# Spectral image tower with a token part: attention on all partitions, column-grouped gate logits, and GpSimd adding up the experts

## The reference

```python
h = ln(h + softmax(q @ k.T / 8) @ v)                   # attention inside one image of 64 tokens
h = ln(h + y1)   # 8 experts of 64-256-64, the best one a token, gate = softmax, capacity 1.25
h = ln(h + mingru(mingru(h)))                           # gated linear recurrence along the 64 rows
h = ln(h + ln(h + y2) * gamma + beta)                   # 16 experts of 64-128-64, the best two a token
```

## Time and profile before

| | us |
|---|---|
| median of three runs | 3008.84 |
| the profiled execution | 3009.09 |
| its span in the profile | 3007.3 |
| token part in the span (2557.6 to 3007.3) | 449.7 |
| TensorE busy in the span | 2714.3 |
| VectorE busy | 2113.5 |
| ScalarE busy | 1992.8 |
| GpSimd busy | 69.6 |

### The profile page before, as it was taken

One profiled execution on the slowest core, in us unless ns is written; L12 is line 12 of the kernel. 1 busy time (PEld: TensorE's weight loads), 2 busy tenths in 40 slices (PEclk: granted clock), 3 DMA queues, 4 the chain that ended last, 5 costly groups with the idle time before them and its releaser, 6 DMA issues.

```text
span 3007.3 us, 75958 instructions
## 1 busy us (share of the span) xinstructions
PE 2714.3 (90%) x28706; PEld 1588.6 (53%) x28706; DVE 2113.5 (70%) x4206; ACT 1992.8 (66%) x2415; POOL 69.6 (2%) x93
## 2 busy tenths in 40 slices
PE   5777789999898999898999879999999999999994
PEld 3444456666666666565666653444444443664441
DVE  5999777888676888676888755445454443677877
ACT  5888666677565777565677546777777777455551
POOL 0000000000000000000000002000000000100000
PEclk9999999999999999999999999999999999989996
DMA  3422255744454744364744344311111110114243
GB/s 93 135 108 106 82 192 171 239 175 174 147 181 153 242 177 174 128 209 156 233 177 177 134 153 90 86 36 60 50 49 58 38 60 0 30 30 102 54 85 64
DMA packets 160241, 361.59 MB, mean 120 GB/s; under 512 B 45878, under 2 KB 123734, under 8 KB 124246
## 3 DMA queue, kind: packets, MB, share of 16 engines
q1 hardware_dynamic: 136982, 185.95, 21.0%
q10 hardware_dynamic: 18432, 134.23, 11.0%
q0 software_dynamic: 4672, 39.20, 6.0%
HBM read 204.77 MB, written 154.53 MB: 119 GB/s over the span
## 4 chain that ended last, share of the span: by engine, by line
PE 74%; DVE 9%; issue 6%; ACT 6%; DMA 4%; SPq 1%; ACTq 0%; DVEq 0%; POOL 0%; POOLq 0%
PE pA L1514 16%; PE pT L1609 8%; PE pA L1522 8%; PE pS L1551 7%; PE pD L1598 5%; PE pD L1565 4%; PE pT L1540 3%; PE pD L1485 3%; PE pD L1580 3%; PE pA L1540 2%; DVE arena L1881 2%; PE pT L1619 2%; ACT h_rows L1698 2%; PE pA L600 2%; DMA h_scratch<-h_new 1%
## 5 line engine op out<-in xcount | busy, mean ns | idle before, releaser
L1848 DVE TENSOR_REDUCE small<-arena 128x32 f32<-128x1056 f32 x320 | 396.7, 1241 | 321.2 <-ACT arena L1683 317.7
L1514 PEld LDWEIGHTS pA<-conv_bd,h_in 128*128 128x128 f32 x4096 | 482.1, 193 | 108.8 <-issue 108.8
L1514 PE MATMUL pA<-conv_bd,h_in 128*128 128x128 f32 x4096 | 520.5, 281 | 3.0 <-DVE arena L1841 1.7
L1673 ACT COPY w_sb<-pA 128x1024 f32<-128x1024 f32 x256 | 259.5, 1014 | 252.7 <-PE pA L1522 235.3
L1694 ACT ACTIVATE h_new<-pT,bet,gam 128x1024 f32<-128x1024 f32 x256 | 307.3, 1200 | 152.7 <-PE pT L1540 135.3
L1862 DVE SCALAR_TENSOR_TENSOR w_sb<-w_sb,small 128x1024 f32<-128x1024 f32 x320 | 385.7, 1209 | 2.1
L1683 ACT ACTIVATE arena<-w_sb 128x1024 f32<-128x1024 f32 x320 | 338.5, 1058 | 10.2
L1551 PEld LDWEIGHTS pS<-cst,h_new 128*128 128x128 f32 x2048 | 220.6, 141 | 203.7 <-issue 133.4
L1540 PE MATMUL pT<-cst,w_sb 128*128 128x128 f32 x2048 | 278.7, 280 | 39.6 <-DVE w_sb L1862 20.0
L1551 PE MATMUL pS<-cst,h_new 128*128 128x128 f32 x2048 | 280.6, 280 | 24.2 <-ACT h_new L1694 21.7
L1540 PEld LDWEIGHTS pT<-cst,w_sb 128*128 128x128 f32 x2048 | 233.5, 144 | 104.4 <-DVE w_sb L1862 48.9
(11 more groups left out here) (316 smaller groups left out, 3421.3 us busy)
## 6 DMA issues: line engine op xcount, KB each, us to landing
h_scratch<-h_new ACTq DMA_DIRECT2D x128, 1024.0 KB, 4.4
h_in<-h_scratch SPq DMA_DIRECT2D x128, 1024.0 KB, 5.0
w_sb<-gates_scratch SPq DMA_DIRECT2D x168, 128.0 KB, 6.9
y_scratch<-w_sb POOLq DMA_DIRECT2D x32, 576.0 KB, 8.5
y_in<-y_scratch SPq DMA_DIRECT2D x512, 36.0 KB
w_sb<-in_L_tok_w1r_dram POOLq DMA_DIRECT2D x8, 576.0 KB, 6.9
w_sb<-in_L_tok_w1i_dram POOLq DMA_DIRECT2D x8, 576.0 KB, 6.7
w_sb<-in_L_tok_w2r_dram POOLq DMA_DIRECT2D x8, 576.0 KB, 7.2
```

Source lines behind the costliest of these rows:

```text
L1514: pe.matmul(pA[:, c:c + 128], h_in[:, 1024 * n + c:1024 * n + c + 128], conv_bd[:], start=(j == 0), stop=False, skip_group_check=True)
L1848: dve.reduce_sum(var[n], sq[n % 2], axis=AX).then_inc(s["summed"], 1)
```

## The change

It does four things. Queries, keys, values and transposed weights are laid on 128 partitions: the two halves of each 128-token tile for queries and keys, even and odd tiles for values and weights, so that each needs 512 columns. Gate logits are computed in a new step `gq` with the gate weights, padded to 32 columns, as the stationary side, in four column groups of 256 columns; ScalarE copies them, and `gl` turns them with two transposes. GpSimd makes the additions of the sum over experts; there are four buffers `Z3`, VectorE waits for a buffer and, ahead of the bias, for the last addition, by a new semaphore `added`; the clear at L891 goes. The list of steps is another one. In `ADDS` the n-th expert in the list has the number of its addition.

```diff
@@ -177,18 +177,18 @@
 TOKEN_ORDER = """
-    xt1.0 qkv.0 xt1.1 sc.0 ex.0 qkv.1 pt.0 xt1.2 pv.0 qkv.2 xt1.3 xt2.0 sc.1 ex.1 sc.2 ex.2 gl1.0 pt.1 gx1.0 pt.2 cum.0 pv.1 qkv.3
-    gt1.0 e1.0 pv.2 e1.0 e1.0 xt2.1 e1.0 xt2.2 e1.0 e1.0 sc.3 gl1.1 e1.0 ex.3 gx1.1 e1.0 eb1.0 pt.3 wg.0 cum.1 gl1.2 yb1.0 pv.3
-    gt1.1 e1.1 e1.1 xt3.0 e1.1 gx1.2 gru0.0 xt2.3 e1.1 gru1.0 e1.1 gback.0 cum.2 e1.1 e1.1 xt4.0 gl1.3 gl2.0 gx2.0 gm2.0 e1.1
-    eb1.1 gt2.0 e2.0 e2.0 e2.0 e2.0 e2.0 e2.0 e2.0 yb1.1 e2.0 e2.0 gx1.3 e2.0 e2.0 xt3.1 e2.0 gru0.1 e2.0 cum.3 gru1.1 gt1.2 e2.0
-    e2.0 e2.0 gt1.3 e1.2 gback.1 e1.2 eb2.0 e1.2 e1.2 yb2.0 e1.2 e1.2 e1.2 e1.2 eb1.2 xt4.1 e1.3 e1.3 yb1.2 e1.3 e1.3 xt3.2 e1.3
-    gru0.2 gl2.1 e1.3 gru1.2 gx2.1 gm2.1 e1.3 gback.2 gt2.1 e1.3 e2.1 eb1.3 xt4.2 e2.1 e2.1 e2.1 yb1.3 e2.1 gl2.2 e2.1 e2.1 xt3.3
-    e2.1 gx2.2 gm2.2 e2.1 e2.1 gru0.3 e2.1 e2.1 e2.1 e2.1 gru1.3 gt2.2 e2.1 e2.1 gback.3 e2.2 e2.2 e2.2 e2.2 e2.2 eb2.1 xt4.3 e2.2
-    e2.2 gl2.3 e2.2 e2.2 e2.2 gx2.3 gm2.3 e2.2 e2.2 e2.2 e2.2 gt2.3 e2.2 e2.2 eb2.2 e2.3 yb2.1 e2.3 e2.3 e2.3 e2.3 e2.3 e2.3 yb2.2
-    e2.3 e2.3 e2.3 e2.3 e2.3 e2.3 e2.3 e2.3 e2.3 eb2.3 yb2.3
+    xt1.0 xt1.1 qkv.0 sc.0 ex.0 qkv.1 pt.0 wg.0 pv.0 sc.1 xt1.2 xt1.3 qkv.2 xt2.0 sc.2 gq1.0 gl1.0 ex.1 pt.1 gx1.0 cum.0 pv.1
+    qkv.3 gt1.0 e1.0 xt2.1 e1.0 gq1.1 e1.0 gl1.1 gx1.1 e1.0 ex.2 e1.0 pt.2 sc.3 e1.0 pv.2 e1.0 e1.0 cum.1 eb1.0 ex.3 xt2.2 pt.3
+    gt1.1 e1.1 yb1.0 e1.1 e1.1 pv.3 gq1.2 xt3.0 e1.1 gru0.0 gl1.2 e1.1 gru1.0 e1.1 gback.0 e1.1 xt2.3 gx1.2 xt4.0 cum.2 gq2.0
+    gq1.3 gl2.0 gx2.0 gm2.0 e1.1 eb1.1 gt2.0 e2.0 e2.0 e2.0 e2.0 e2.0 gl1.3 e2.0 yb1.1 gx1.3 cum.3 gt1.2 e2.0 e2.0 e2.0 e2.0 xt3.1
+    e2.0 e2.0 gru0.1 e2.0 e2.0 e2.0 gru1.1 e2.0 eb2.0 e1.2 e1.2 yb2.0 e1.2 e1.2 e1.2 gback.1 gt1.3 e1.2 e1.2 e1.2 eb1.2 xt4.1 e1.3
+    e1.3 yb1.2 e1.3 e1.3 xt3.2 e1.3 gru0.2 gq2.1 e1.3 gru1.2 gl2.1 e1.3 gx2.1 gm2.1 e1.3 gback.2 gt2.1 e2.1 e2.1 e2.1 eb1.3 xt4.2
+    e2.1 e2.1 e2.1 gq2.2 e2.1 e2.1 e2.1 gl2.2 e2.1 gx2.2 yb1.3 e2.1 e2.1 e2.1 gm2.2 e2.1 xt3.3 e2.1 e2.1 gt2.2 gru0.3 e2.2 e2.2
+    e2.2 gru1.3 e2.2 e2.2 e2.2 gback.3 e2.2 e2.2 e2.2 e2.2 xt4.3 e2.2 e2.2 gq2.3 e2.2 gl2.3 eb2.1 gx2.3 gm2.3 e2.2 e2.2 e2.2 gt2.3
+    eb2.2 e2.3 e2.3 e2.3 yb2.1 e2.3 e2.3 e2.3 e2.3 yb2.2 e2.3 e2.3 e2.3 e2.3 e2.3 e2.3 e2.3 e2.3 e2.3 eb2.3 yb2.3
 """
-TOKEN_SENDS = dict(xt1=(0, 2), qkv=(4, 2), sc=(1, 0), pt=(0, 2), pv=(1, 0), xt2=(2, 0), xt4=(2, 0), gl1=(1, 0), gl2=(1, 0), cum=(1, 0),
+TOKEN_SENDS = dict(xt1=(0, 2), qkv=(2, 1), sc=(1, 0), pt=(0, 1), pv=(2, 0), xt2=(2, 0), xt4=(2, 0), gq1=(0, 1), gq2=(0, 1), gl1=(1, 0), gl2=(1, 0), cum=(1, 0),
                    wg=(0, 1), gt1=(0, 1), gt2=(0, 1), eb1=(1, 0), eb2=(1, 0), xt3=(0, 2), gru0=(1, 1), gru1=(1, 1), gback=(1, 0),
                    yb1=(1, 0), yb2=(1, 0),
...
-        b2a, b2b, ge2 = param(P, S), param(P, S), param(P, 512)
+        b2a, b2b, ge2, z3c, z3d = param(P, S), param(P, S), param(P, 512), param(P, 512), param(P, 512)
-        gwa, gwb = param(P, E1), param(P, E2)
+        gwa, gwb = param(P, 32), param(P, 32)
...
-        QT, KT, VB, PT = ([arena[0:64, 2048 * i + 1024 * j:2048 * i + 1024 * j + 1024] for j in range(2)] for i in range(4))
+        QT, KT, VB, PT = ([arena[:, 1024 * i + 512 * j:1024 * i + 512 * j + 512] for j in range(2)] for i in range(4))
-        Z3 = [w_sb[:, 2 * CW + CW * i:3 * CW + CW * i] for i in range(2)]
+        Z3 = [w_sb[:, 2 * CW + CW * i:3 * CW + CW * i] for i in range(2)] + [z3c, z3d]
...
+        LG = [y_in[:, 512:768], cst[:, 128:384]]
-        GT_PLACE, EB_FREED, sends_d = {}, {}, 0
+        GT_PLACE, EB_FREED, ADDS, sends_d = {}, {}, [], 0
+            if key[0] in ("out1", "out2"):
+                ADDS.append(ADDS[-1] + (key[2] > 0) if ADDS else -1)
...
             def qkv(c):
                 pe.wait_ge(s["ones_set"], 2)
                 taken("s", "xt1", c)
-                for j in range(2):
-                    for which, w in (("d", wq), ("s", wk)):
-                        b = bank(which)
-                        sent(which, pe.matmul(b[0:64, :], w, XT[:, 1024 * c + 512 * j:1024 * c + 512 * j + 512], start=True, stop=True))
-                for j in range(2):
-                    b = bank("d")
-                    for i in range(8):
-                        a = 1024 * c + 512 * j + S * i
-                        mm = pe.matmul(b[0:64, S * i:S * i + S], XT[:, a:a + S], wv, start=True, stop=True)
-                    sent("d", mm)
+                for which, w in (("d", wq), ("s", wk)):
+                    b = bank(which)
+                    x = XT[:, 1024 * c:1024 * c + 1024].rearrange("p (t h q) -> p h t q", h=2, q=S)
+                    for h in range(2):
+                        mm = pe.matmul(b[64 * h:64 * h + 64, :].rearrange("p (t q) -> p t q", q=S), w, x[:, h], start=True, stop=True)
+                    sent(which, mm)
+                b = bank("d")
+                for m in range(4):
+                    for h in range(2):
+                        for u in range(2):
+                            a = 1024 * c + 256 * m + 128 * u + 64 * h
+                            q = 128 * m + 64 * h
+                            mm = pe.matmul(b[64 * u:64 * u + 64, q:q + 64], XT[:, a:a + S], wv, start=True, stop=True)
+                sent("d", mm)
             def sc(c):
                 taken("d", "qkv", c)
...
-                        a = 128 * i + 64 * h
-                        mm = pe.matmul(b[64 * h:64 * h + 64, S * i:S * i + S], QT[c % 2][:, a:a + 64], KT[c % 2][:, a:a + 64], start=True, stop=True)
+                        q, a = slice(64 * h, 64 * h + 64), slice(S * i, S * i + S)
+                        mm = pe.matmul(b[q, a], QT[c % 2][q, a], KT[c % 2][q, a], start=True, stop=True)
             def pt(c):
-                for j in range(2):
-                    b = bank("s")
-                    for i in range(4):
-                        t = CT * c + 4 * j + i
-                        mm = pe.transpose(b[0:64, 128 * i:128 * i + 128], Sx[:, S * t:S * t + S], ident)
-                    sent("s", mm)
+                b = bank("s")
+                for m in range(4):
+                    mm = pe.transpose(b[:, 128 * m:128 * m + 128], chunk(Sx, c)[:, 128 * m:128 * m + 128], ident)
+                sent("s", mm)
             def pv(c):
-                b = bank("d")
-                for i in range(CT):
-                    for h in range(2):
-                        a = 128 * i + 64 * h
-                        mm = pe.matmul(b[64 * h:64 * h + 64, S * i:S * i + S], PT[c % 2][:, a:a + 64], VB[c % 2][:, a:a + 64], start=True, stop=True)
-                sent("d", mm)
+                for u in range(2):
+                    b = bank("d")
+                    rows = slice(64 * u, 64 * u + 64)
+                    for m in range(4):
+                        for h in range(2):
+                            a = 128 * m + 64 * h
+                            mm = pe.matmul(b[64 * h:64 * h + 64, S * m:S * m + S], PT[c % 2][rows, a:a + 64], VB[c % 2][rows, a:a + 64], start=True, stop=True)
+                    sent("d", mm)
             def wg(c):
...
-            def logits(E, gw, split):
+            def logits(gw, split):
                 def step(c):
+                    b = bank("s")
+                    for j in range(4):
+                        a = 1024 * c + 256 * j
+                        mm = pe.matmul(b[32 * j:32 * j + 32, 0:256], gw, XT_split[:, a:a + 256], start=True, stop=True)
+                    sent("s", mm)
+                return step
+            def turn_logits(layer):
+                def step(c):
+                    taken("s", f"gq{layer}", c)
-                    for i in range(CT):
-                        t = CT * c + i
-                        mm = pe.matmul(b[:, E * i:E * i + E], XT_split[:, 128 * t:128 * t + 128], gw, start=True, stop=True)
+                    for i in range(2):
+                        mm = pe.transpose(b[:, 128 * i:128 * i + 128], LG[layer - 1][:, 128 * i:128 * i + 128], ident)
...
             def qkv(c):
-                for j in range(2):
-                    act.copy(KT[c % 2][:, 512 * j:512 * j + 512], take()[0:64, :]).then_inc(s["ts_free"], 1)
+                act.copy(KT[c % 2], take()[:]).then_inc(s["ts_free"], 1)
             def ex(c):
             def pt(c):
-                for j in range(2):
-                    act.copy(PT[c % 2][:, 512 * j:512 * j + 512], take()[0:64, :]).then_inc(s["ts_free"], 1)
+                act.copy(PT[c % 2], take()[:]).then_inc(s["ts_free"], 1)
             def upper(c):
+            def keep_logits(layer):
+                def step(c):
+                    act.copy(LG[layer - 1], take()[:, 0:256]).then_inc(s["ts_free"], 1)
+                return step
             def gx1(c):
...
             def qkv(c):
-                for j in range(2):
-                    dve.tensor_copy(QT[c % 2][:, 512 * j:512 * j + 512], take()[0:64, :]).then_inc(s["td_free"], 1)
-                for j in range(2):
```

(35 more changed lines are left out.)

12 lines of the change are left out of this document (6 added, 6 removed).

## The result

The changed kernel takes 3025.6 us (median of 8 runs, 3017.0 to 3031.5), the kernel before 3009.9 us on the same chip (3002.4 to 3014.2): ratio 1.0063, 95% interval 1.0048 to 1.0077. (The two medians lie 15.7 us apart, 0.52%, which the interval holds; this text goes by the ratios.) It is slower by 0.63%, 19 us, where the prediction had 2986 us, faster by 0.8%, with a range that ended at 3004. The profiled execution took 3024.16 us, span 3022.2. The spectral part is as it was (the token part begins at 2556.8, before 2557.6); the token part takes 465.4 us where it took 449.7.

The account below looks back on a forecast made before the run. TensorE was taken to bound the token part up to the last gate transpose, VectorE the end. Terms summed to -24.8 us, -22.8 after 2 given back for late gates: from 3009.1, less 0.25, to 2986 us; range 2963 to 3004.

Parts of the forecast that it names:

- two experts of chunk 2 ahead of gt2.3: New list: two experts moved before the last gate transpose put 3.9 us more TensorE work ahead of it.
- gates that come a little late: Gates delayed behind GpSimd's additions, twice a microsecond: 2 us given back in the sum.
- Behind both stand 4 banks of products and 4 buffers for sums, so while TensorE bounds, nothing: New waits, of VectorE's bias for GpSimd's last addition and of gate stores behind additions, were claimed to cost nothing.
- The late stores: Rival, chance 0.10: gate stores queue behind GpSimd's additions, 16 us, plus 4 for bias waits; 3006 us, no change.
- Attention and gate logits: Token part: fewer or paired TensorE products save 12.4 us in attention and 9.4 us in gate logits.
- My own last sentence: Sign: forecast wrong as a whole if TensorE's idle time in the middle grows as much as its work shrinks.
- clock: Around a gate-logit step: fewer narrow products return TensorE's granted clock, 0 to 8 us, taken as 4.
- The additions' relief: Middle of the token part: additions leaving VectorE relieve TensorE's waits behind it, 5 of 15.3 us.
- The port: GpSimd's additions hold VectorE at the shared port: 2 us in the end; as rival, chance 0.10, 36 us, 3022.
- The bias waits: VectorE's bias addition waits for GpSimd's last addition, 1.36 us, eight times; counted as nothing while TensorE bounds.
- the price of an addition: One addition on GpSimd, between 1.13 and 1.31 us, taken as 1.26, or 1.36 with its semaphores.
- the end stretch: From the last gate store to the span's end: 86.9 us, 1.2 more than before, with GpSimd slower than VectorE.

Follow-up runs that it names:

- e3: The kernel before with the new attention and gate logits alone (old list, additions on VectorE): 0.9973 of the kernel before, 3001.2 us.
- e1: The changed kernel with the 88 additions back on VectorE, new list kept: 1.0049 of the kernel before, 3023.2 us.
- e2: The changed kernel with the old list of steps (new logit steps put in), additions on GpSimd: 0.9977 of the kernel before, 3001.4 us.
- e10: The changed kernel with the gates of the second layer's chunks 1 to 3 one to two experts earlier in its list: 1.0037 of the kernel before.
- e13: The changed kernel with the second layer's gates of chunks 1 to 3 earlier and the gate stores issued by ScalarE: 0.9994 of the kernel before.
- e4: The changed kernel with each gate store issued by ScalarE right behind its copy, not by GpSimd: 1.0009 of the kernel before, 3010.9 us.
- e5: The changed kernel with one part of its list, from gq2.2 to eb2.2, put back to the old order: 1.0046 of the kernel before, 3020.8 us.
- e11: The changed kernel with the new list up to eb1.2 and the old list from there: 0.9995 of the kernel before.
- e7: The kernel before with the new attention steps alone: 0.9980 of the kernel before.
- e8: The kernel before with the new column-grouped gate logits alone: 0.9989 of the kernel before.
- e6: The changed kernel with the old list and the gate stores issued by ScalarE, additions on GpSimd: 0.9957 of the kernel before, 2991.7 us.

## Why the prediction was wrong

**The step that failed is the list.** I priced it as "two experts of chunk 2 ahead of gt2.3" (3.9 us in the sum), plus 2 us for gates that come a little late. The runs put the list at 0.76% with VectorE's additions (e3 to e1) and 0.86% with GpSimd's (e2 to the changed kernel), 23 and 26 us. I had read it as a row of TensorE's work, when a number to read in it was how many experts stand between a chunk's gates (gm2) and its first product: 2, 8 and 6 for chunks 1, 2 and 3 of the second layer in the old list, 1, 3 and 3 in the new one, and none of them behind gt2 in place of 1, 2 and 2. Moving an expert from one side of a gate to the other takes no work away; what it takes away is cover for the gates' trip. Timeline of e2 (the old list), to be held against the one of the kernel after:

```profile
2857.99 0.29 DVE L994 TENSOR_TENSOR arena<-w_sb 128x128 f32<-128x128 f32 x1
2866.90 0.33 PE L627 MATMUL pS<-cst,arena 128*128 128x128 f32 x1
...
2870.24 0.56 POOL L1040 DMA_DIRECT2D gates_scratch<-h_in  x1
2881.43 0.69 DVE L908 TENSOR_TENSOR h_new<-pA,w_sb 128x512 f32<-128x512 f32 x1 [1.96 <-DMA w_sb<-gates_scratch]
```

Here the gates are ready 23.2 us before the first product (16.1 in the kernel after), and VectorE waits 1.96 us where it waits 8.88. The trip from store to product, where VectorE waits for it, took 9.4 to 12.5 us in the second layer, over all traces (11.1 and 11.2 us for chunk 2 in these two); what differs is the work beside it.

How much of the list's cost is this distance is shown only in part. Putting the gates earlier gave 0.26% of the 0.86% (e10), and 0.15% with the stores on ScalarE (e13 to e4). In the traces, TensorE's waits for first products grew by 12 us where the token part grew by 21 (e2 to the changed kernel), and with VectorE's additions by 6 us of 17 (4.2 in e3, 10.1 in e1). The rest stays open. Part of it lies between eb1.2 and gq2.2 or at yb2.1 (e5 to e11). What the first half of the new list costs (0.18 to 0.25%) no run here explains; the trace of the changed kernel has one new wait there, TensorE's for VectorE's gate choice of chunk 3 ahead of the cumulative step, 3.29 us, which the old list does not have. That is argued, not shown.

**"Behind both stand 4 banks of products and 4 buffers for sums, so while TensorE bounds, nothing"** failed with it. The late stores were the rival with 0.10, and its price, 16 us, is what e4 gave back. That the two sizes agree is partly luck: the rival had six stores 2.7 us late, the trace has five that are 1.4 to 6.4 us late, and e4 takes away GpSimd's wait for the landing as well. Its counter-argument, that TensorE must itself pass those experts before the transpose, overlooked that GpSimd passes them after VectorE, which runs behind TensorE.

**Attention and gate logits** were mis-sized in what reaches the path. TensorE's busy time fell by 13.8 us in e7 and 11.4 in e8, against 12.4 and 9.4. On the time they are 6 and 3 us. "Up to the last gate transpose (gt2.3, 2920.5) the kernel is therefore bound by TensorE" was the reading behind it: a TensorE that is busy for 95% of the stretch was taken for one whose work is the path for 95% of it. My own last sentence named what would make the forecast wrong as a whole, TensorE's idle time growing as its work shrinks, and e3 shows it in good part (12 of 19.6 us). The **clock**'s 4 us no run isolates: the mean over the token part is 0.91 before and in e3, and 0.92 in e7 and e8, of which only e8 has the new logits.

These two steps failed independently. The forecast was 22.8 us below the kernel before and the result is 19 above it, 42 us apart. The list took some 20 us more than its terms, and all that e2 holds gave 7 us (0.23%) where the sum had some 30. With the list priced right and nothing else, the forecast would have been 2986 + 20 = 3006 us, still past the end of the range.

**The additions' relief**, 5 us in the middle: with the stores out of the way it is 0.07% in the old list, 2 us, not told from nothing, and 0.30% in the new one, 9 us. **The port**: the hold is there, and its 3 us on the time are not told from nothing. **The bias waits** came to 7.8 us in the middle and 5.7 in the end. By themselves they make no kernel slower than the one before: in e6, which is faster than both kernels, they stand at 14.7 us.

**What held:** the price of an addition, 1.285 us, inside the bounds of 1.13 and 1.31 (though the upper one doesn't follow from its rows: four times 0.30 is 1.20); the multiplications at 0.69 us beside them; and the end stretch, from the last store to the span's end: 87.1 us, where I had 86.9.

## What to carry to other kernels

A hand-written order is part of the kernel's timing and has to be priced by distances and not by work alone: for each round trip (here some 11 us through DRAM) count how much work stands between its start and its first use, before and after. Here TensorE's waits at such first uses grew by 12 us where the order cost 21 with the additions on GpSimd, and by 6 where it cost 17 with them on VectorE. An engine that takes on compute should not keep a queue that others wait for: the stores moved to ScalarE gave 0.54% in the new list where GpSimd had additions (0.20% in the old one) and 0.1% where it had none. An engine busy for 95% of a stretch is not yet the bound; take work off it in an experiment, and see what becomes idle.
